# The last three sequences' rest of a second layer, cut into pieces between its first nine expert tiles

## What is computed

```
x  = x + retention_0(x);  x = norm(x);  x = x + experts_0(x)   (top 2 of 8, F = 256)
x  = norm(x)
x  = x + retention_1(x);  x = norm(x);  x = x + experts_1(x)   (top 2 of 8, F = 512)
```

## Time and profile before

| | us |
|---|---|
| median of 3 runs | 1245.91 (1244.36 to 1247.92) |
| profiled execution | 1238.92 |
| its span | 1237.1 |
| busy in the span: PE, DVE, ACT, POOL | 1118.3, 905.7, 743.7, 730.9 |

### The profile page before, as it was taken

One profiled execution on the slowest core, in us unless ns is written; L12 is line 12 of the kernel. 1 busy time (PEld: TensorE's weight loads), 2 busy tenths in 40 slices (PEclk: granted clock), 3 DMA queues, 4 the chain that ended last, 5 costly groups with the idle time before them and its releaser, 6 DMA issues.

```text
span 1237.1 us, 31542 instructions
## 1 busy us (share of the span) xinstructions
PE 1118.3 (90%) x10358; PEld 1000.2 (81%) x10358; DVE 905.7 (73%) x2660; ACT 743.7 (60%) x2015; POOL 730.9 (59%) x900
## 2 busy tenths in 40 slices
PE   6999999995489999978999999976899999999992
PEld 5788888884379999956777777755799999999992
DVE  4788898888467777756868888864676666667873
ACT  2335544652356877755656777753566666666884
POOL 0247777775477777661456667566744444445775
PEclk9999999997699999999989999995999999999996
DMA  8212111211144333442222111011311121113454
GB/s 247 63 59 74 47 39 53 74 32 47 39 118 135 103 108 105 123 152 86 84 85 64 51 62 49 31 42 49 98 58 57 55 59 56 56 56 124 148 182 122
DMA packets 75424, 101.78 MB, mean 82 GB/s; under 512 B 15138, under 2 KB 51490, under 8 KB 74850
## 3 DMA queue, kind: packets, MB, share of 16 engines
q1 hardware_dynamic: 49538, 59.89, 16.9%
q0 software_dynamic: 17280, 35.69, 8.6%
q10 hardware_dynamic: 8448, 4.20, 1.1%
HBM read 59.87 MB, written 43.04 MB: 83 GB/s over the span
## 4 chain that ended last, share of the span: by engine, by line
PE 56%; DVE 21%; ACT 7%; issue 6%; POOL 5%; DMA 3%; SPq 1%; ACTq 0%; DVEq 0%; POOLq 0%
PE banks L2231 16%; PE banks L2250 10%; PE banks L1346 6%; PE banks L1364 4%; DVE a_sT L1062 3%; DVE b_sT L1997 2%; PE banks L1298 2%; PE banks L1268 2%; DMA scattered<-b_r_x,b_r_idx 2%; ACT a_r_x L253 2%; PE banks L1295 1%; PE banks L349 1%; PE banks L1314 1%; DVE a_qm L1169 1%; PE banks L2215 1%
## 5 line engine op out<-in xcount | busy, mean ns | idle before, releaser
L1748 POOL DMA_INDIRECT expert_out<-e_ysb,b_e_idx x142 | 161.6, 1138 | 152.5 <-ACT e_ysb L1854 123.5
L2231 PE MATMUL banks<-b_e_x_hi,e_w_hi 128*128 128x256 f32 x568 | 167.2, 294 | 3.9 <-ACT e_sgl L1844 2.3
L872 POOL DMA_INDIRECT expert_out<-a_e_ysb,a_e_idx x142 | 142.3, 1002 | 42.9 <-issue 33.6
L2231 PE MATMUL banks<-b_e_x_hi,e_w_lo 128*128 128x256 f32 x568 | 160.3, 282 | 0.0
L470 POOL DMA_INDIRECT scattered<-a_r_x,a_r_idx x128 | 129.7, 1013 | 36.3 <-issue 36.3
L2250 PE MATMUL banks<-w_dn,e_h 128*128 x1136 | 138.3, 275 | 2.3 <-DVE e_h L2043 1.6
L2250 PEld LDWEIGHTS banks<-w_dn,e_h 128*128 128x128 f32 x1136 | 132.5, 192 | 3.1 <-issue 3.1
L2043 DVE TENSOR_TENSOR e_h<-banks,e_sgl 128x512 f32<-128x512 f32 x142 | 97.0, 689 | 50.6 <-PE banks L2231 48.0
L1844 ACT ACTIVATE e_sgl<-banks 128x512 f32<-128x512 f32 x142 | 85.0, 599 | 75.1 <-DVE e_h L2043 44.0
L470 POOL DMA_INDIRECT scattered<-b_r_x,b_r_idx x112 | 110.7, 989 | 31.0 <-issue 31.0
L2031 DVE TENSOR_TENSOR e_w_lo<-w_gu,e_w_hi 128x1024 fp32r<-128x1024 f32 x71 | 87.1, 1227 | 53.6 <-ACT e_w_hi L1833 53.6
(11 more groups left out here) (374 smaller groups left out, 3282.8 us busy)
## 6 DMA issues: line engine op xcount, KB each, us to landing
a_e_xg<-scattered SPq DMA_DIRECT2D x71, 130.0 KB
b_e_xg<-scattered SPq DMA_DIRECT2D x71, 130.0 KB
b_cy<-expert_out SPq DMA_DIRECT2D x32, 256.0 KB
f_y<-expert_out SPq DMA_DIRECT2D x32, 256.0 KB, 3.8
a_xT<-in_x_T SPq DMA_DIRECT2D x16, 256.0 KB, 2.9
out<-f_x ACTq DMA_DIRECT2D x16, 256.0 KB, 2.7
expert_out<-a_e_ysb,a_e_idx POOLq DMA_INDIRECT x142, 2.3
expert_out<-e_ysb,b_e_idx POOLq DMA_INDIRECT x142
```

The source lines that it names most:

```text
L872: nc.gpsimd.indirect_dma_start(out=expert_out, out_offset=bass.IndirectOffsetOnAxis(ap=idx[n % HELD][:, i:i + 1], axis=0), in_=ysb[n % HEL ...
L1748: nc.gpsimd.indirect_dma_start(out=expert_out, out_offset=bass.IndirectOffsetOnAxis(ap=idx[n % 4][:, i:i + 1], axis=0), in_=ysb[n % 4][:, ...
L2231: mm = nc.tensor.matmul(bank_of(c, j)[:, i * ROWS:(i + 1) * ROWS], w_[c % RING][:, g, f:f + P], x_[c % RING][:], start=(m == 0), stop=(m = ...
```

## The change

`UNITS`, `slot_units` and `fill` go. Steps end at 18 (`LAST_STEP`), and `ALONE` is 9. What steps 19, 20 and 21 did is written out as pieces, placed in front of or behind `unit(u)` for u from 0 to 8, on each engine. Nothing is added to the computation and nothing taken away: each engine has the same instructions in another order, and the banks of tiles 3 to 8 and the waits on them are others. The tables for the later tiles (`second_counts` and its followers), which hang on `ALONE`, move back by six units too.

```diff
                 n_w = 16 * len(early)
 
 
-                UNITS = {(19, 1): 1, (20, 1): 1, (21, 4): 1}
                 CENTRING = 10
-                ALONE = sum(UNITS.values())
-
-                def slot_units(s, point):
-
-                    first = sum(n for at_, n in UNITS.items() if at_ < (s, point))
-                    return range(first, first + UNITS.get((s, point), 0))
+                ALONE = 9
+                LAST_STEP = SEQS + 3
+                t12, t13, t14, t15 = (turn(0, n, 0, SEQS, 2) for n in (12, 13, 14, 15))
 
...
-                    for s in range(AHEAD, SEQS + 7):
-                        def fill(point):
-                            for u in slot_units(s, point):
-                                unit(u)
-                        step(s, fill)
-                    for u in range(ALONE, STEPS + DRAIN):
+                    for s in range(AHEAD, LAST_STEP):
+                        step(s)
+                    norm.power(pool, t14)
+                    scatter_all(t12)
+                    router.put_places(pool, t13)
+                    scatter_all(t13)
+                    norm.power(pool, t15)
+                    router.put_places(pool, t14)
+                    scatter_all(t14)
+                    for u in range(STEPS + DRAIN):
                         unit(u)
+                        if u == 7:
+                            router.put_places(pool, t15)
+                            scatter_all(t15)
                         if u in CLOSING:
...
 
-                    def step(s, fill):
+                    def root_rows(c1):
+                        act.wait_ge(root.chain.sem, InverseRoot.LINKS * c1.n + InverseRoot.LINKS)
+                        wait_count(act, ex_mm, c1.n)
+                        nc.scalar.copy(yb[:].rearrange("p (n d) -> p n d", d=DH1),
+                                       root.y[:].unsqueeze(2).to_broadcast([P, CH * H1, DH1])).then_inc(yb_there, 1)
+
+                    def late_turned_rows(d, bank):
+                        act.wait_ge(router.tp, d.n + 1)
+                        nc.scalar.copy(router.xT[:], bank[:, :]).then_inc(router.xT_there, 1)
+
+                    def late_rows(c2):
+                        router.wait_free(act, c2)
+                        act.wait_ge(x3_kept, c2.n - 1)
+                        norm.apply(act, r, router.copy_of(0, c2)[:, :, 0:D], c2, x3_there)
+
...
-                    for s in range(AHEAD, SEQS + 6):
-                        def fill(point):
-                            for u in slot_units(s, point):
-                                unit(u)
-                        step(s, fill)
-                    for u in range(ALONE, STEPS + DRAIN):
+                    for s in range(AHEAD, LAST_STEP):
+                        step(s)
+                    norm.squares(act, r, t14, r_there)
+                    for u in range(STEPS + DRAIN):
+                        if u == 1:
+                            late_turned_rows(t13, T1)
+                            late_rows(t14)
+                            late_copies(t13)
+                        if u == 3:
+                            late_turned_rows(t14, T0)
+                            late_copies(t14)
+                        if u == 5:
+                            late_rows(t15)
+                        if u == 6:
+                            late_turned_rows(t15, T0)
+                            late_copies(t15)
                         unit(u)
+                        if u == 1:
+                            root_rows(t15)
+                            router.tanh_of(act, t13)
+                        if u == 4:
+                            norm.squares(act, r, t15, r_there)
+                            router.tanh_of(act, t14)
+                        if u == 7:
+                            router.tanh_of(act, t15)
                         if u in CLOSING:
                             closing(CLOSING[u])
...
                         nc.vector.memset(vz[i][:], 0.0).then_inc(zero_there, 1)
-                    for s in range(AHEAD, SEQS + 6):
-                        def fill(point):
-                            for u in slot_units(s, point):
-                                unit(u)
-                        step(s, fill)
-                    for u in range(ALONE, STEPS + DRAIN):
+                    for s in range(AHEAD, LAST_STEP):
+                        step(s)
+                    residual(t14)
+                    for u in range(STEPS + DRAIN):
+                        if u == 1:
+                            choose(t13)
+                            variance_root(t15)
+                        if u == 2:
+                            router.rows_of(dve, RK, t13)
+                            tables.middle(dve)
+                            scaled(t15)
+                        if u == 4:
+                            choose(t14)
+                            residual(t15)
+                        if u == 5:
+                            router.rows_of(dve, RK, t14)
+                        if u == 7:
+                            choose(t15)
+                        if u == 8:
+                            router.rows_of(dve, RK, t15)
                         unit(u)
                         if u == ALONE + 2:
                             tables.second_counts(dve)
...
                             mm.then_inc(kt_mm, 1)
-                        fill(4)
                         if d:
                             router.ranks_mm_(pe, RK, d)
 
-                    for s in range(AHEAD, SEQS + 6):
-                        def fill(point):
-                            for u in slot_units(s, point):
-                                unit(u)
-                        step(s, fill)
-                    for u in range(ALONE, STEPS + DRAIN):
+                    for s in range(AHEAD, LAST_STEP):
+                        step(s)
+                    for u in range(STEPS + DRAIN):
+                        if u == 0:
+                            pe.wait_ge(router.xT_there, t12.n + 1)
+                            pe.wait_ge(r_there, t13.n + 1)
+                            project_out(t14)
+                            pe.wait_ge(x3_there, t13.n + 1)
+                            pe.wait_ge(oT_there, t14.n + 1)
+                            router.transposes(pe, T1, router.copy_of(0, t13)[:, :, 0:D], t13)
+                        if u == 1:
+                            router.logits_mm(pe, LG, t13)
+                            variances(t15)
+                        if u == 2:
+                            router.ranks_mm_(pe, RK, t13)
+                            spread_roots(t15)
+                        if u == 3:
+                            pe.wait_ge(x3_there, t14.n + 1)
+                            pe.wait_ge(r_there, t14.n + 1)
+                            router.transposes(pe, T0, router.copy_of(0, t14)[:, :, 0:D], t14)
+                        if u == 4:
+                            router.logits_mm(pe, LG, t14)
+                            project_out(t15)
+                        if u == 5:
+                            router.ranks_mm_(pe, RK, t14)
+                        if u == 6:
+                            pe.wait_ge(x3_there, t15.n + 1)
+                            pe.wait_ge(r_there, t15.n + 1)
+                            router.transposes(pe, T0, router.copy_of(0, t15)[:, :, 0:D], t15)
+                        if u == 7:
+                            router.logits_mm(pe, LG, t15)
+                        if u == 8:
+                            router.ranks_mm_(pe, RK, t15)
                         unit(u)
 
         early_places = {}

```

More of the change, by code:

```diff
@@ L1772, in paced, with scatter_all, step @@
                                 router.scatter_pair(pool, e, 3)
-                    def step(s, fill):
+                    def scatter_all(t):
+                        for q in range(4):
+                            router.scatter_pair(pool, t, q)
+                    def step(s):
                         _, y, a, b, c1, c2, d, e = turns(s, lags + [7])
@@ L2282, in step @@
                         if c1:
[L2284 to L2291 removed]
+                            variances(c1)
                         if a:
```

116 lines of the change are left out of this document (37 added, 79 removed).

## The result

The changed kernel takes 1247.73 us (median; 1241.28 to 1250.52). The kernel before, run beside it and again since, has a median of 1241.7 us (1237.7 to 1247.92); the three runs that the prediction started from had given 1245.91, high in that range. The ratio of after to before is 1.0041, 95% interval 1.003 to 1.0052: about 5 us slower, a little more than the 0.3% that I had set as the bound of "within". The predicted 1247.5 lies beside the measured median by luck: the start was 4.2 too high, and the change cost some 5 where I had 1.6, so two errors of about the same size cancelled.

What follows compares the result with a forecast made beforehand. TensorE's list was taken as the bound, judged by unit 14's start: 13.2 us won, 7.6 and 6.2 lost, 0.6 later (4.2 with a late clock). Taking 1.6 on 1245.91 gave 1247.5 us, range 1241.0 to 1254.0.

Steps and rivals of the forecast that it cites:

- within: Whole kernel: time less than 0.3%, 3.7 us, from no change; chance 0.56.
- The start: Whole kernel: median of 1245.91 us before the change, to which the forecast added 1.6 us.
- Handover: Sequence 14's output projection to unit 5's start: earlier units win 13.2 us, or 9.6 with the clock still low.
- My sign for being wrong: Start of unit 5: the forecast is wrong if it comes after 868; predicted 864.1.
- Banks: Units 5 to 13: one set of banks for longer makes TensorE wait, a loss of 7.6 us.
- Pieces in the units 5 to 8: Moved pieces ahead of `w_hi` or `w_lo` delay TensorE; four units take 30.6 us, a loss of 6.2.
- The sum: Start of unit 14: 0.6 us later with the clock early, 4.2 with it late; 1.6 taken.
- Rival 1: Clock stays low through unit 5: plus 6.5 to 7 us, about 1252.7; chance 0.21.
- Its own point of decision: Sequence 15's projection, about 855: clock not back before it means above 0.3% slower.
- Rival 2: Units 5 to 8: pieces hidden in waits, 6.1 us each, 6.2 less in all, 1241.3; chance 0.12.
- Rival 3: Units 5 to 11: waits on the single bank set drop the clock, plus 23 us, 1269; chance 0.03.
- Rival 4: Unit 12: late GpSimd stores make `ysb` wait, plus 2 to 5 us, 1250; chance 0.08, shared with omitted hops.

Runs made afterwards that it cites:

- the kernel with this edit alone: Kernel before with only tiles 3 to 8 kept to one set of banks, nothing moved; ratio to the kernel before 1.0098 (1.0076 to 1.012).

## Why the prediction was right or wrong

- **The start.** I added the change to a median of 1245.91, of three runs that had fallen high; the longer series has 1241.7. From there my 1.6 would have given 1243.3, 4.4 below the measured time; only the high start put the forecast beside it. The forecast of "within 0.3%" was wrong, by a little: 0.41%. That the profiled execution lies 7.0 below the median "for both" was wrong too: after's lies 1.1 above it.
- **Handover: 13.2 won with the clock early, 9.6 with the clock late.** Measured 10.4. With fillers ahead, and the clock up from unit 3 on, unit 5 starts at 37.9 to 38.2; I had 864.1 - 824.39 = 39.7. The walk along the new order was right to 2 us, and its main waits are there: 3.02 for `xT`, 2.96 for the root, 1.78 for the SiLU of unit 3. What failed is the sentence "I take 1.6, nearer to the early clock, because TensorE has matmuls nearly without a gap from 839.9 on now". It had not: it waited 2.96 at 839.6. The clock came back only in unit 2, and after the waits of 1.78 and 0.54 in unit 3 it was lost again at 855, just ahead of the longest dense piece, the projection of 15. I had priced a clock that comes late, but not one that comes and goes. My sign for being wrong, unit 5 after 868, reads 869.59 in the profile, and 866.9 without the 2.73 ahead of D.
- **Banks: 7.6.** Right in D: 7.6 without the 0.7 of table work, and the units 9 to 13 of after took 30.2 where I had 30.1. The time of the kernel with this edit alone says more, as told above.
- **Pieces in the units 5 to 8: 7.3, 9.0, 7.9, 6.4, in sum 30.6.** After has 8.1, 9.9, 9.4, 6.9, in sum 34.3, and with the clock at 1.00 7.9, 8.8, 8.0, 6.9, in sum 31.6. So 1.0 is my sizing (unit 5 and 8 each some 0.5 short), 2.7 in this execution the clock, which I had as full from unit 5 on. The waits are where I put them: for the SiLU in unit 6, for `h` in unit 7 (2.30).
- **The sum.** With all fillers the changed kernel has a D of 99.9 against 99.6 to 99.8 for before, and a ratio of 1.0002: nothing, as the early-clock sum said (+0.6), which took before as it is, at its low clock. The term that was mis-sized is the clock: I gave it 1.0 between +0.6 and +4.2. In D it was 7.1 (4.3 in the handover and 2.7 in the units 5 to 8), nearly all of the 7.2; in the time 4.8, the difference of 1.0041 and 1.0002.
- **Rival 1, clock low, +6.5 to 7, 1252.7.** This is nearest to what happened; from a start of 1241.7 its price gives 1248.5, beside the measured 1247.73. Its own point of decision, that the clock is not there for the projection of 15, was met; its price lay in other places than I put it, in part in the units 6 to 8.
- **Rival 2, pieces hidden.** No: 31.6 for four units at full clock, not 24.4.
- **Rival 3, the single set makes the clock fall.** No. In the units 9 to 13 TensorE waits 0.7 to 0.8 in each, and the clock is 1.00 for 29 us; so too with one set in the kernel before. The rule of the Trainium skill ("TensorE: Matmul & The Clock Gate", section "A second HAM failure mode: psum-queue depth-cycling") doesn't agree with this trace, in which going through a few banks with short waits kept the clock. The clock did go up and down in the units 3, 6 and 7, where the waits for the same banks are longer, 1.8 to 2.3 us, because a piece stands ahead of the SiLU or of `h` that frees the bank; and with the copies behind, the clock fell in unit 3 behind waits of 1.18 and 0.56.
- **Rival 4, GpSimd late.** No: units 12 and 13 take 5.88 each, and no wait in them is above 0.8.

What stays open: what decides whether the clock survives such a wait. In single profiles the same waits kept it once and lost it once, it was lost once behind waits of 1.18 and 0.56, and fillers didn't prevent a fall in one unit 6 and in the kernel before. Open too: which of the early fillers holds it, how the clock's price divides between the handover and the units 5 to 8, and what before would take with its own clock held up.

## What to carry to other kernels

Where a reordering breaks TensorE's list into portions, sum the schedule once at each clock, and ask of each long dense piece what stands right ahead of it: here the clock, lost just ahead of the longest projection and again later, cost 4.8 us in the time and 7.1 in D, as much as the single set of banks (7.6) or the pieces (6.2 by my sum). When pieces of other work go between tiles, put on each engine first what the tile's products hang on and what is only stored away behind it, and tie each bank to the last use of that bank and not to one common point: these two and fillers in the long waits turned a loss of 0.4% into a gain of 0.3 to 0.6%. Look at such a change by the distance between two points that both kernels share, since the part of the program ahead moved by 2.7 us from one execution to the next by itself; but where the clock comes and goes take more than one profile of it, and hold it against the times: one execution here was 3.0 us faster than the median of its kernel.

## What the runs showed of the hardware

- In the changed kernel the granted clock rose in the products of unit 2, at 848 (a product took 0.41 us at 847.79 and 0.28 at 848.33), and the products are at 1.2 GHz again from 855.20 on, behind waits of 1.78 and 0.54; it stayed at 0.50 to 865.20, although TensorE was busy for all of these 10.00 us (window above).
- The same waits (1.8 and 2.3 us the longest) lost the clock in one execution (0.72 and 0.76) and kept it at 1.00 for 31.80 us in another, whose handover had fillers.
- 24 small bf16 matmuls took 1.5 to 2.7 us in the waits, 8 took 0.62. In the changed kernel they took 7.1 us off D (4.8 in the time); in the kernel before they left the clock at 0.59 and 0.50 in the dense parts and took 1.0 off D.
